# A four-layer transformer on one core: the order of the first steps, of the conditioning work and of the first layer's query rotations is changed

## The reference

```python
# layer 0: RMS norm scaled by the condition, attention with rotary q and k, gated MLP
h = n(x) * (w * (1.0 + cond @ tw.T)); q, k, v = h @ Wq.T, h @ Wk.T, h @ Wv.T   # 8 heads of 64, one k/v head
x = x + softmax(rope(q) @ rope(k).T / 8) @ v @ Wo.T
x = x + silu(h2 @ Wg.T) * (h2 @ Wu.T) @ Wd.T
# layer 1: layer norm with shift and scale from silu(cond), attention on normalised q and k, GELU MLP
# layer 2: layer norm with shift and scale from cond, rotary attention with a latent k/v and a sparse mask
# layer 3: 8 experts on slices of 64 features, layer norm with silu(emb), output product
```

## Time and profile before

| | |
|---|---|
| Median of 3 runs | 2158.23 us (2153.22 to 2158.89) |
| The profiled execution | 2151.35 us, its span 2149.6 us |
| TensorE busy | 1930.4 us, 90% of the span |
| VectorE, ScalarE, GpSimd busy | 1132.2, 1029.0, 785.8 us |
| Mean granted TensorE clock | 0.953 of full speed |

### The profile page before, as it was taken

How to read it: one execution, slowest core, us unless ns; L and a number is a source line. 1 busy time by engine, 2 the same in 40 slices (tenths; PEclk the granted TensorE clock), 3 DMA queues, 4 the chain that set the end, 5 groups by cost and what they waited for, 6 DMA issues and landing times.

```text
span 2149.6 us, 34826 instructions
## 1 busy us (share of the span) xinstructions
PE 1930.4 (90%) x12744; PEld 1512.8 (70%) x12744; DVE 1132.2 (53%) x3157; ACT 1029.0 (48%) x2450; POOL 785.8 (37%) x1093
## 2 busy tenths in 40 slices
PE   4778999999999999999899999979999989977875
PEld 2556777777888878788678777768875768745453
DVE  4656432653553365435674675574554675456442
ACT  3533332343333344443465465555567456477753
POOL 4454553211112443233577453336331432233220
PEclk9889999999999999999899999999999989989988
DMA  7234666545445533345345433424433424322310
GB/s 264 64 128 147 216 206 225 191 157 188 163 173 180 184 133 127 133 157 196 133 167 174 156 123 133 149 91 151 141 118 128 163 80 171 120 77 79 98 60 30
DMA packets 95097, 310.35 MB, mean 144 GB/s; under 512 B 10576, under 2 KB 11344, under 8 KB 93392
## 3 DMA queue, kind: packets, MB, share of 16 engines
q1 hardware_dynamic: 94928, 308.12, 41.4%
HBM read 241.50 MB, written 66.58 MB: 143 GB/s over the span
## 4 chain that ended last, share of the span: by engine, by line
PE 65%; DVE 13%; issue 7%; ACT 6%; POOL 6%; DMA 2%; SPq 0%; POOLq 0%; DVEq 0%; ACTq 0%
PE B L183 59%; PE B L186 6%; DVE SS L207 2%; DVE FB L204 2%; DMA ST<-in_wpack 2%; ACT SS L189 2%; POOL SS L198 1%; ACT FB L189 1%; POOL W L201 1%; POOL R L201 1%; DVE T L201 1%; DVE PT L195 1%; DVE FB L201 1%; ACT L189 1%; POOL W L198 1%
## 5 line engine op out<-in xcount | busy, mean ns | idle before, releaser
L198 POOL TENSOR_SCALAR SS<-SS,NM 128x256 f32<-128x256 f32 (+1 forms) x640 | 290.0, 470 | 829.4 <-DVE NM L213 829.3
L183 PE MATMUL B<-HM,W 128*128 128x512 f32 x2304 | 538.6, 394 | 15.6 <-DVE HM L204 8.7
L183 PEld LDWEIGHTS B<-HM,W 128*128 128x128 f32 x2304 | 438.8, 191 | 110.3 <-DVE HM L204 9.5
L183 PE MATMUL B<-G,W 128*128 128x512 f32 x1536 | 404.0, 414 | 29.7 <-DVE FB L204 9.8
L183 PEld LDWEIGHTS B<-G,W 128*128 128x128 f32 x1536 | 292.9, 196 | 103.9 <-issue 20.8
L189 ACT ACTIVATE SS<-SS,NM 128x256 f32<-128x256 f32 (+1 forms) x512 | 240.6, 471 | 218.1 <-DVE NM L198 217.8
L183 PE MATMUL B<-HA,W 128*128 128x512 f32 x864 | 222.3, 408 | 7.9 <-DVE HA L201 5.9
L186 PE MATMUL B<-ident,SS 128*128 128x128 f32 x1152 | 179.2, 294 | 40.3 <-POOL SS L198 27.8
L183 PEld LDWEIGHTS B<-HA,W 128*128 128x128 f32 x864 | 165.6, 196 | 46.9 <-DVE HA L201 6.3
L186 PEld LDWEIGHTS B<-ident,SS 128*128 128x128 f32 x1152 | 129.8, 147 | 76.1 <-POOL SS L198 34.2
L201 DVE TENSOR_TENSOR G<-FB,G 128x512 fp32r<-128x512 f32 x128 | 101.3, 793 | 155.2 <-ACT G L189 155.1
(11 more groups left out here) (108 smaller groups left out, 2658.7 us busy)
## 6 DMA issues: line engine op xcount, KB each, us to landing
W<-kept SPq DMA_DIRECT2D x357, 512.0 KB, 4.3
kept<-W SPq DMA_DIRECT2D x119, 512.0 KB, 4.6
ST<-in_wpack SPq DMA_DIRECT2D x135, 256.0 KB, 3.0
Y<-in_adaw SPq DMA_DIRECT2D x12, 1024.0 KB, 6.4
out_xT<-X SPq DMA_DIRECT2D x16, 256.0 KB, 2.1
X<-in_xT SPq DMA_DIRECT2D x1, 3072.0 KB, 14.6
FB<-in_pos SPq DMA_DIRECT2D x4, 256.0 KB, 7.6
X<-in_xT SPq DMA_DIRECT2D x1, 1024.0 KB, 6.7
```

Of the source, the lines that this page charges most:

```text
L183: return self.real.matmul(*a, **k) if self.real is not None else self
L198: return self.real.tensor_scalar(*a, **k) if self.real is not None else self
```

## The change

The step list is changed in these ways; no instruction's arithmetic is.

- x of chunk 0 comes in four transfers of 256 KB, one for each c, each with a semaphore of its own, and the square of slice c waits for its own transfer. They are issued ahead of CT. rotm is issued after the first two stage loads (step "load rot").
- "start" no longer holds silu(cond) and the exp; they are in a step "cond" at position 6, and ScalarE waits for CT only there. The first groups of ada use the plain condition, and wait for its transfer and not for silu.
- "nsub", "nsq" and "nvar" of the first norm come directly after one another; the step "trig" (ScalarE's sines, VectorE's last angle step) comes after "adt". Weight slots are given out from step 6 of the list on instead of step 4, and two stage loads are issued before. With these, GpSimd's queue holds two splits ahead of the first power instead of four.
- The load of the other chunks of x (3 MB) comes after the first "kv" instead of before it. The first "v" moves in position, but keeps its place in the list.
- `q0` becomes [-0.458, 2.946]: ro2 and qs of a layer 0 query tile at s + 2.946 instead of s + 0.467 (15 tiles, all but the first). The second tile has 0.049 less. So scores, normalise, turn and softmax of units 0 and 2 stand ahead of the second tile's rotation.
- `k0`: the kv product of chunks 1 to 3 at s - 0.054 instead of s + 0.377, which is ahead of the scores at s; its last part at s + 3.267 instead of s + 2.72.
- Small moves of norms, out, up, positions and ada around units 3 to 29.

```diff
-    "q0": [-0.458, 0.467],
-    "k0": [0.377, 2.321, 1.654, 2.72],
+    "q0": [-0.458, 2.946],
+    "k0": [-0.054, 2.321, 1.654, 3.267],
...
+    "start": [-14.853, 6, -2.831, -0.049],
...
-        self.over(self.trig(0), [b, b + 0.1, b + 0.2, b + 0.3])
+        self.over(self.trig(0), [b, b + 0.2, b + 0.21, b + 1.9])
         self.at(b + 0.05, self.add, "start")
...
         self.at(b + 0.06, self.add, "load ada", 0)
-        self.over(self.stats(("a", 0, 0)), [b + 1, b + 1, b + 2])
-        self.over(ada[0], [b + 2.1, b + 2.2])
+        self.at(b + 0.07, self.add, "load rot")
+        self.over(self.stats(("a", 0, 0)), [b + 1, b + 1, b + 1.01])
+        self.over(ada[0], [b + 1.1, b + 1.2])
         self.over(self.final(("a", 0, 0)), [b + 3])
-        self.at(b + 4, self.add, "load x")
+        self.at(PLACE["start"][0], self.add, "load x")
+        self.at(PLACE["start"][1], self.add, "cond")
...
-            while w < len(self.uses) and s > 3:
+            while w < len(self.uses) and s > 5:
...
-                    e.wait_ge(*a_silu.of())
+                    e.wait_ge(*(a_silu.of() if which else s_ct.of()))
...
                     e.dma_start(CV[:, :], cols).then_inc(*s_cv.up())
+                    for c in range(4):
+                        e.dma_start(X[:, c, 0:512], xT[:, c, 0:512]).then_inc(*s_x0[c].up())
                     e.dma_start(CT[:, 0, :, :], condT).then_inc(*s_ct.up())
-                    e.dma_start(X[:, :, 0:512], xT[:, :, 0:512]).then_inc(*s_x0.up())
                     e.dma_start(ident[:, :], consts[0]).then_inc(*s_id.up())
+                elif kind == "load rot":
                     e.dma_start(rotm[:, :], consts[1]).then_inc(*s_rot.up(0))
```

More of the change, by code:

```diff
@@ L35 @@
     "m final": [19.93, 36.106, 52.069, 68.347, 84.611, 99.748, 122.714, 149.431],
[2 rows of a table removed]
-    "trig": [3.589, 19.977, 35.517],
-    "out": [17.499, 33.857, 49.401, 65.605, 81.749, 97.151, 113.474, 129.833, 145.534, 161.861, 177.973, 194.882],
[2 rows of a table added]
+    "trig": [3.589, 19.817, 35.517],
+    "out": [17.616, 33.857, 49.401, 65.605, 81.749, 97.151, 113.474, 129.833, 145.534, 161.861, 177.973, 194.882],
     "first": [137.43, 168.366, 179.31, 201.305],
@@ L60 @@
     "down": [0.802],
-    "ada": [6.238, 22.32, 25.596, 28.55, 31.373, 34.773, 37.512, 39.248, 43.72, 46.196, 49.144],
+    "start": [-14.853, 6, -2.831, -0.049],
+    "ada": [7.098, 22.32, 25.596, 28.723, 31.373, 34.773, 37.512, 39.248, 43.72, 46.196, 49.144],
 }
@@ L402, in projections @@
         s = 16 * ITEM[L, n] + 4 * t - 4 - AHEAD
-        s += 1 if L == 1 and t == 0 else 0
+        s += 1 if L == 1 and t == 0 else PLACE["start"][3] if (L, n, t) == (0, 0, 1) else 0
         q, k, v = (PLACE[x + str(L)] for x in "qkv")
@@ L497, in make @@
         self.at(b + 0.06, self.add, "load ada", 0)
-        self.over(self.stats(("a", 0, 0)), [b + 1, b + 1, b + 2])
-        self.over(ada[0], [b + 2.1, b + 2.2])
+        self.at(b + 0.07, self.add, "load rot")
+        self.over(self.stats(("a", 0, 0)), [b + 1, b + 1, b + 1.01])
+        self.over(ada[0], [b + 1.1, b + 1.2])
         self.over(self.final(("a", 0, 0)), [b + 3])
-        self.at(b + 4, self.add, "load x")
+        self.at(PLACE["start"][0], self.add, "load x")
+        self.at(PLACE["start"][1], self.add, "cond")
         self.over(self.projected("k", 0, 0, 0), [b + 5, b + 7])
         self.over(self.projected("q", 0, 0, 0), [b + 6, b + 7.5])
-        self.at(b + 8, self.value, 0, 0, 0)
+        self.at(PLACE["start"][2], self.value, 0, 0, 0)
         for i in range(1, ADA_GROUPS):
@@ L623, in spread @@
         for s, step in enumerate(steps):
-            if step[0] == "load x":
+            if step[0] == "load rot":
                 load()
                 load()
-            while w < len(self.uses) and s > 3:
+            while w < len(self.uses) and s > 5:
                 if self.plain(w):
@@ L717, in program @@
         weights = Weights(plan.steps)
-        s_const, s_x0, s_x, s_pos, s_tab, s_out = (tally(x, 16) for x in (
-            "s_const", "s_x0", "s_x", "s_pos", "s_tab", "s_out"))
+        s_const, s_x, s_pos, s_tab, s_out = (tally(x, 16) for x in (
+            "s_const", "s_x", "s_pos", "s_tab", "s_out"))
+        s_x0 = [tally(f"s_x0_{c}", 16) for c in range(4)]
         s_st = [tally(f"s_st{k}", 16) for k in range(STAGES)]
@@ L751, in program @@
         tallies = [
-            s_const, s_x0, s_x, s_pos, s_tab, s_out, *s_st, s_ad, s_cv, s_ct, s_id, s_rot, p_adt, d_ad, *s_w, p_ada, p_tot, p_var, p_bc, p_qkv, p_rot, p_ss,
+            s_const, *s_x0, s_x, s_pos, s_tab, s_out, *s_st, s_ad, s_cv, s_ct, s_id, s_rot, p_adt, d_ad, *s_w, p_ada, p_tot, p_var, p_bc, p_qkv, p_rot, p_ss,
             p_nb, p_sc, p_tr, p_va, p_out, p_up, p_down, p_first, p_second, p_last, a_silu, a_sm, a_sq,
@@ L775, in source, with source_ready @@
             return lambda c: X[:, c, 512 * n:512 * n + 512]
-        def source_ready(i):
+        def source_ready(i, c=3):
             kind, L, n = i
@@ L785, in source_ready @@
                 return d_xd.of(4 * L - 4 + n, 3, 3)
-            return s_x.of() if n else s_x0.of()
+            return s_x.of() if n else s_x0[c].of()
         def target(i, c):
@@ L878, in tensor @@
                     e.wait_ge(*s_ad.of(i))
-                    e.wait_ge(*a_silu.of())
+                    which = 1 if 2 <= i < 8 or i >= 10 else 0
+                    e.wait_ge(*(a_silu.of() if which else s_ct.of()))
                     e.wait_ge(*dp.over(u))
-                    which = 1 if 2 <= i < 8 or i >= 10 else 0
                     for c in range(4):
@@ L1115, in vector @@
                 kind, a = step[0], step[1:]
-                if kind == "start":
+                if kind == "cond":
                     e.tensor_scalar(SM[:, :], CV[:, COLS["sml"]:COLS["sml"] + 4], math.log(100.0), None,
@@ L1398, in scalar @@
         def scalar(e):
-            e.wait_ge(*s_ct.of())
             e.wait_ge(*s_cv.of())
@@ L1403, in scalar @@
                 kind, a = step[0], step[1:]
-                if kind == "start":
+                if kind == "cond":
+                    e.wait_ge(*s_ct.of())
                     e.activation(CT[:, 1, :, :], CT[:, 0, :, :], ACT.Silu).then_inc(*a_silu.up())
@@ L1414, in scalar @@
                         else:
-                            e.wait_ge(*source_ready(i))
+                            e.wait_ge(*source_ready(i, c))
                         if i in norm_before:
```

## The result

The changed kernel takes 2127.16 us (median of 4 runs, 2125.18 to 2128.53) against 2156.1 (2153.22 to 2158.89, 4 runs) for the kernel before. The ratio is 0.9879, with the 95% interval from 0.9864 to 0.9894: 1.2% or 29 us faster, where about 16 were forecast. Its profiled execution took 2125.18 us with a span of 2123.4, 26.2 less than that of before. One line added to its helpers shifts their numbers: L184 is the matmul, L187 the transposition, L190 the activation, L199, L202 and L205 the vector operations.

What follows compares the result with a forecast made beforehand. TensorE, busy 90% of the span, was taken as the bound, with its idle time early. Gains of 5.0 + 1.5 + 2.1 + 2.0 + 5.5 = 16.1 us against a 2155.4 mean gave 2139 us, range 2126 to 2153.

Steps and rivals of the forecast that it cites:

- The head: Start up to the first projection: power at 16.4 instead of 21.97 us; gain 5.0 us, bounds 4.4 to 5.6.
- transfers do not overlap: Rival at the start: x's four transfers run one after another, head's gain lost, 2144 us; chance 0.05.
- x late: Rival at the start: x comes no earlier, but the stage's landing paces the power; forecast time stays; chance 0.07.
- The first scores' exchange: Unit 0's turn: first scores ahead of the second rotation leave 2.1 us idle instead of 3.67, gaining 1.5 us.
- The stalls at 70.80 and 87.48: TensorE stalls of 2.96 and 3.54 us with rotation work ahead: moving rotations gains 2.1 and 2.0 us.
- The stalls from 110 to 220: Four TensorE stalls, 13.6 us in all, with rotations ahead on VectorE: gain 5.5 us, bounds 0 to 8.3.
- What stood behind them: Exp, angles or the norm's last part may be late next; not shown by the trace, no separate cost given.
- the clock comes back too: Rival from 48 to 220 us: removed stalls take slow-clock spells with them, 8 to 12 us more, 2129; chance 0.15.
- kv and the small moves: Three kv products one step earlier, ahead of the scores, queue else the same: 0 us, bounds -2 to +2.
- The condition: Silu, exp and two table loads at unit 6, 3.1 us on ScalarE, covered by its idle time: cost 0.
- The stalls only move: Rival from 48 us: rotations delay the next unit's reciprocal as much, only the head is gained, 2150; chance 0.13.
- Scores wait for Q lo: Rival, slower: scores wait 1.2 to 2.2 us in each of 15 tiles; 2169 at 2 us; chance 0.05.

Runs made afterwards that it cites:

- after: The changed kernel with all edits, against the kernel before the change: 2127.16 us, ratio 0.9879.
- before: The kernel without the change: 2156.1 us, median of 4 runs; its profiled execution took 2151.35 us.
- e3: Changed kernel with all positions from the first projections on put back, keeping only the new start and the condition at unit 6: 2149.12 us, ratio 0.9975.
- e4: Changed kernel with chunk 0's x in one 1 MB transfer instead of four: 2131.14 us, ratio 0.9898 to the kernel before.
- e5: Changed kernel with four splits instead of two ahead of the first power: 2132.19 us, ratio 0.9901 to the kernel before.
- e6: Changed kernel with GpSimd's splits from the third on held until the first norm's last subtraction: 2128.32 us, ratio 0.9878 to the kernel before.
- e8: Changed kernel with the first attention norm at 3.951 instead of 3.377, behind the next product again: 2132.00 us, ratio 0.9898 to the kernel before.
- e9: Changed kernel with k0 (kv product of chunks 1 to 3) put back: 2130.45 us, ratio 0.9899 to the kernel before.
- e10: Kernel before the change with only the new q0 (rotations) and new k0 (kv): 2136.81 us, ratio 0.9926.
- e7: Changed kernel with the condition's silu and exp back at the start, behind the squares, instead of unit 6: 2126.38 us, ratio 0.9872 to the kernel before.
- e1: Kernel before the change with only the rotations moved, to s + 2.946 from s + 0.467: 2139.08 us, ratio 0.9932.
- e2: Changed kernel with only the rotations put back to s + 0.467: 2146.77 us, ratio 0.9970 to the kernel before.
- e12: Changed kernel with layer 0 query products at s - 1.2 instead of s - 0.458, rotations still at s + 2.946: 2156.49 us, ratio 1.0021 to the kernel before.
- e11: Changed kernel with the rotations at s + 1.9 instead of s + 2.946: 2161.00 us, ratio 1.0043 to the kernel before.

## Why the prediction was right in its direction and short in its size

It forecast 2139 with a range from 2126 to 2153; the time is 2127.2, at the range's lower end. Step by step:

- **The head, 5.0: right**, 5.1 at the first scores, or 4.7 by the means over the profiles with either start. That it fits to 0.1 is luck, since its parts do not: the power 6.1 earlier (5.6 forecast; the stage landed at 11.98, not 12.45), less 1.4 of contention in the norm, where 0.6 was taken and 1.2 was the bound, then 0.4 back before the scores. The table load did not start with CV at 4.33, as the working said, but at 5.51 with x. The rivals "transfers do not overlap" and "x late" are out: the squares ended at 8.99.
- **The first scores' exchange, 1.5: right**, 3.67 to 2.07, where 2.1 was said to remain.
- **The stalls at 70.80 and 87.48, 2.1 and 2.0:** 1.8 (2.96 gone, 1.18 new one turn earlier) and 3.2 went. But near the first a wait of 2.4 us for the norm's sum came, which the norm's own move had put ahead of the product.
- **The stalls from 110 to 220, 5.5:** 2.17, 2.97, 4.57 and 3.86 became 0.27, 1.34 (at another turn), 2.02 and 2.88, together 7.1 less, inside the bounds of 0 to 8.3. All idle time over the same work went from 19.9 to 15.8 us, 4.1 less where the prediction named 5 as its sign. With the first turn and two stalls the rotations' terms said 11.1; the three kinds of wait fell by 11.4.
- **What stood behind them, taken at nothing: wrong by 6 us.** Waits for T, FB, the exp and Q lo took 6.6 of the 11.4 back, so that the idle time of the stretch fell by 5.1.
- **The sum as idle time alone: the step that failed.** The largest term, 10.1 us of busy time at a granted clock of 0.94 instead of 0.86, was not in it. It stood among the rivals as "the clock comes back too", 8 to 12 us more, 2129, with a chance of 0.15; that is the case that came. The reason given against it, that shorter stalls remain in each unit, was true of the stalls and no reason for the clock: the twelve matmuls of a scores step take 0.99 us in after behind a wait of 2.88 us. The clock in the earlier trace rows, 0.83 and 0.87 in the two stretches that the change touches and 1.00 where TensorE is full, was the number to put in the sum. With before and e3 on one side and the four profiles of one order (after, e4, e5, e6) on the other, the means differ by 7.6 us of busy time and 5.8 of idle time; so 10.1 is the high end, and the clock's part is more than half in either case.
- **The 12 us by which the forecast was off.** The two errors of opposite sign, 6 and 10 us, leave 4. Another 6 lie outside the head and the stretch, where the prediction counted nothing, and 2 come from comparing medians with the two profiled executions (29 us by the one, 26 by the other, from a base of 2156.1 and not 2155.4).
- **kv and the small moves, 0 with ±2: probably too small.** By the medians kv is worth 2 to 3 us and the norm's move 5 (e8, e9, e10), with intervals that overlap.
- **The condition, 0: right** (e7, within the noise).
- **"The stalls only move": refuted** by e1 and e2. Some did, at a smaller size, and e8 shows one doing so.
- **"Scores wait for Q lo": did not decide**, 0.9 us once in the stretch instead of over 1.1 in each tile. e12 shows that the mechanism is real once the product that covers the chain is gone, at a price above the one given.

In total, 26.2 us of span are 5.1 in the head, 15.1 in the stretch, 2.9 from 216 to 428 us and 3 behind 829 us. Of the 2.9, 2.2 are idle time that went, by no edit that was tested; the last 3 are not explained: from 428 to 829 us the lead is constant at about 23, and behind it the kernels of the study differ among themselves by as much, without an edit there. Nor is it settled why the same idle time goes with different clocks: e10 has 30.4 us idle in the stretch, a little less than after's 30.8, and a clock of 0.89 against 0.94; e5 has 28.6 and 0.89 with the order of steps of after. That fewer stalls bring the clock back is shown by e1, e2, e11 and e12 as a whole, whose differences are far above these; which stall sets it off is not.

## What to carry to other kernels

When stalls go from a stretch in which the granted clock is below full, add to their idle time the busy time that the clock would give back; here that was more than half of the stretch's gain, and the whole gain was lost again with one position set wrongly (e11, e12). Take such a stretch from more than one profile: with one and the same order it differed by 4 us. Long work of one item belongs behind the short steps that others wait for, and directly ahead of a long step of the bound engine that covers it; test the cover by moving it away. Then look at who waits at the places that were freed, for more than half of the idle time that went came back under other names (6.6 of 11.4 us).

## What the runs showed of the hardware

- The clock, in one pair of windows around the turns of units 16 and 17, which do not hold quite the same work, first of before, then of after (length, busy times, clock): with 1.7 us idle of 8 the granted clock is 0.57, with 0.5 us idle it is 1.00.

```profile
126.00:134.00 8.00, 6.28 (x30) 4.85 (x31) 4.53 (x14) 3.61 (x13) 3.53 (x7) 0.57 0.00 0
```

```profile
114.00:122.00 8.00, 7.46 (x46) 5.68 (x45) 4.71 (x13) 4.14 (x15) 5.33 (x8) 1.00 0.02 9
```

- The same order and the same waits (2.07 and 0.8 us) were followed by a product of 12 matmuls that took 2.99 us in after and 5.39 in e5.
- A VectorE subtraction of 128x512 with both inputs in SBUF took 0.69 us alone and up to 1.2 (2.44 for two) beside a GpSimd split, and a GpSimd operation of 1.27 us took 1.58.
- A table load was followed by its user after 0.01 us, twice.
- Four transfers of 256 KB, issued within 1.86 us, let the first reader start at 5.51 us, where one of 1 MB let it start at 7.60.
- The first twelve matmuls of the first projection took 4.5 to 5.5 us from profile to profile with the recorded clock at 1.00; twelve of the same shape took 2.99 us at 50.46 in after.
